# Routed experts of a decoder layer: scattering with accumulation into the output, and both experts' weights staged

## The reference

```python
scores = sigmoid(x @ router)                 # 16 experts, groups of 4, two groups kept
topk_indices = top 2 of scores + e_bias within the two groups
topk_weights = scores[topk] / sum(scores[topk])
a = relu2(x @ w_up[e]) * combine[:, e]       # 512 -> 256
routed = sum over e of a @ w_down[e]         # 256 -> 512
shared = relu2(x @ shared_up) @ shared_down  # 512 -> 1024 -> 512
out = x_residual + routed + shared
```

## Time and profile before

| | |
|---|---|
| Time, median of 3 runs | 1128.84 us (1126.65 to 1132.16) |
| Profiled execution, its own time | 1128.89 us |
| Its span, first to last instruction | 1127.2 us |
| Mean granted TensorE clock | 0.987 |
| Busy: TensorE, VectorE, ScalarE, GpSimd | 94%, 75%, 60%, 58% |
| DMA, mean over the span | 82 GB/s |
| Last down projection of the tile loop ends | 1089.04 us |

### The profile page before, as it was taken

How to read it: one execution, slowest core, us unless ns; L and a number is a source line. 1 busy time by engine, 2 the same in 40 slices (tenths; PEclk the granted TensorE clock), 3 DMA queues, 4 the chain that set the end, 5 groups by cost and what they waited for, 6 DMA issues and landing times.

```text
span 1127.2 us, 19610 instructions
## 1 busy us (share of the span) xinstructions
PE 1060.9 (94%) x6786; PEld 620.4 (55%) x6786; DVE 845.7 (75%) x1297; ACT 676.8 (60%) x1492; POOL 656.7 (58%) x573
## 2 busy tenths in 40 slices
PE   8999988888999999999989889999999999999993
PEld 3554556666666667666666654544444445555541
DVE  6988699999999999999999989840680045545548
ACT  4876789999999899999999944412011022333310
POOL 2022299999999999999999955202043024444420
PEclk9999989999999999999999999999999999999997
DMA  7210001102111111010221007112225523333329
GB/s 225 94 39 21 21 29 39 37 31 76 34 34 30 39 67 39 30 38 31 84 75 31 20 23 278 38 74 75 75 75 206 167 81 122 122 112 123 108 76 381
DMA packets 50865, 92.95 MB, mean 82 GB/s; under 512 B 9294, under 2 KB 17486, under 8 KB 50768
## 3 DMA queue, kind: packets, MB, share of 16 engines
q1 hardware_dynamic: 44368, 72.82, 19.4%
q0 software_dynamic: 6400, 18.88, 5.2%
HBM read 72.67 MB, written 19.01 MB: 81 GB/s over the span
## 4 chain that ended last, share of the span: by engine, by line
PE 71%; POOL 8%; DVE 7%; ACT 7%; issue 5%; DMA 1%; SPq 0%; DVEq 0%; ACTq 0%; POOLq 0%
PE ps L1570 10%; PE ps L2017 7%; PE ps L2029 6%; PE ps L843 6%; POOL w_all L765 5%; PE ps L1584 5%; PE ps L871 4%; PE ps L358 4%; PE ps L832 4%; PE ps L817 4%; DVE w_all L1042 3%; PE ps L310 3%; PE ps L1593 2%; ACT w_all L956 2%; PE ps L882 2%
## 5 line engine op out<-in xcount | busy, mean ns | idle before, releaser
L765 POOL TENSOR_TENSOR w_all<-w_all 128x512 f32<-128x512 f32 x256 | 320.7, 1272 | 20.1 <-DVE w_all L587 14.8
L1042 DVE TENSOR_TENSOR_SCAN w_all<-ps,w_all 128x512 f32<-128x512 f32 x256 | 298.6, 1205 | 1.2 <-ACT ps L939 0.6
L939 ACT ACTIVATE ps<-w_all,low 128x512 f32<-128x512 f32 x256 | 177.6, 697 | 1.0 <-DVE w_all L1042 0.8
L871 PE MATMUL ps<-ident,w_all 128*128 128x128 f32 x1024 | 162.0, 281 | 9.7 <-DVE acc L1050 9.5
L947 ACT ACTIVATE w_all<-ps,low 128x128 f32<-128x128 f32 (+3 forms) x256 | 132.8, 530 | 13.6 <-DVE low L1034 13.6
L871 PEld LDWEIGHTS ps<-ident,w_all 128*128 128x128 f32 x1024 | 114.9, 142 | 34.7 <-issue 20.8
L956 ACT ACTIVATE w_all<-ps 128x256 f32<-128x256 f32 (+2 forms) x192 | 101.9, 531 | 22.9 <-PE ps L832 22.6
L1034 DVE TENSOR_REDUCE low<-ps 128x2 f32<-128x256 f32 (+3 forms) x128 | 103.8, 811 | 14.6 <-PE ps L817 13.9
L1570 PE MATMUL ps<-w_all 128*128 128x512 f32 x256 | 112.1, 594 | 0.0
L832 PE MATMUL ps<-ident,w_all 128*128 128x128 f32 x640 | 108.8, 285 | 1.5 <-ACT low L1013 1.5
L843 PE MATMUL ps<-w_all,low 128*32 128x128 f32 x1280 | 95.0, 278 | 12.1 <-ACT w_all L956 10.8
(11 more groups left out here) (228 smaller groups left out, 1935.2 us busy)
## 6 DMA issues: line engine op xcount, KB each, us to landing
w_all<-b_scratch SPq DMA_DIRECT2D x64, 256.0 KB, 3.2
w_all<-in_w_up SPq DMA_DIRECT2D x16, 512.0 KB, 6.0
w_all<-in_w_down SPq DMA_DIRECT2D x16, 512.0 KB, 7.1
w_all<-sorted_y SPq DMA_DIRECT2D x16, 512.0 KB, 10.5
norms<-attn SPq DMA_DIRECT2D x4, 1024.0 KB, 4.3
out_dram<-acc SPq DMA_DIRECT2D x16, 256.0 KB, 8.8
attn<-in_x SPq DMA_DIRECT2D x3, 1024.0 KB, 6.0
attn<-in_x SPq DMA_DIRECT2D x12, 256.0 KB, 4.3
```

Source lines behind the costliest of these rows:

```text
L765: pool.tensor_tensor(dbu[:, k, :], keep["du"][i // N][:, k * T:(k + 1) * T], b_all[i % 2][:, :], ALU.mult).then_inc(pool_dbu.sem, pool_dbu ...
L871: last = pe.transpose(yb[which][:, k * P:(k + 1) * P], state[i % 2][:, k, t * P:(t + 1) * P], ident[:, :])
L939: act.activation(da[unit % 2][:, :], keep["dt"][i // N][:, k * T:(k + 1) * T], ACT.Exp, scale=keep["a_flat"][:, unit % (N * KD):unit % (N ...
L1042: dve.tensor_tensor_scan(state[i % 2][:, k, :], da[unit % 2][:, :], dbu[:, k, :], 0.0, ALU.mult, ALU.add).then_inc(dve_scan.sem, dve_scan. ...
```

## The change

The output is now written in two steps. First SP stores `acc` (residual and shared experts) of each batch to the output, four transfers of 1 MB, one after another (`store`). Then the y tiles are added to it by GpSimd's accumulating indirect DMAs. Since one tile may hold both pairs of a token, each tile has two scatters: `add_first` adds the rows whose expert is the token's lower one, `add_second` the others, and rows that are not meant are pointed out of bounds. A second scatter waits until the first one of its tile has landed. The late matmuls' result is copied by ScalarE to `acc` of the last batch and added by four plain accumulating DMAs of GpSimd.

The routing weight is now applied to y, as the scale of ScalarE's copy. For that the router sends each pair's weight through the one-hot product too, split into three bf16 pieces (three more planes in `inverse`, a second set of 32 matmuls in `collect`, more small operations in `choose` and `tokens`).

Both units' weights are now staged at fixed places: ScalarE copies the first expert's up weights (with a register load of its own), VectorE the second's up weights and both experts' down weights, with two register loads. TensorE loads no registers. There are four x buffers and four y buffers instead of two of each. Four x loads are issued before the loop instead of two.

```diff
+            def store(b):
+                sp.wait_ge(dve_base.sem, dve_base.upto(4 * b + 3))
+                if b > 0:
+                    sp.wait_ge(s_out.sem, s_out.upto(b - 1))
+                sp.dma_start(d["out"][b, :, :].rearrange("(t p) c -> p t c", p=P),
+                             keep["acc"][:, b, :].rearrange("p (t c) -> p t c", c=D)).then_inc(s_out.sem, s_out.tick(b))
...
             expert(6)
             expert(8)
+            store(0)
...
             expert(11)
+            store(1)
             sp.wait_ge(r["s_routed"], 1)
...
             expert_down(10)
+            store(2)
+            store(3)
             routed["sync"](sp)
...
             pool.wait_ge(s_keep.sem, s_keep.upto(B - 1))
-            for i in range(2):
-                pool.indirect_dma_start(out=r["x_first"][:, i, :], out_offset=None, in_=d["norm_rows"],
+            pool.wait_ge(s_out.sem, s_out.upto(0))
+            for i in range(4):
+                pool.indirect_dma_start(out=r["x_in"][i], out_offset=None, in_=d["norm_rows"],
...
+        for w in range(3):
+            self.link(dve, dve.tensor_tensor(self.weights[:, :, w, :], self.in_tile[:, :, :], over(self.piece[:, w, :], NI), ALU.mult))
         dve.tensor_tensor(self.in_row, over(self.row[:, :], P), each(self.row_id[:, :], P), ALU.is_equal).then_inc(self.s_inverse, 1)
...
-        load(2)
-        load(3)
+        def add_second(i):
+            pool.wait_ge(s_first[i % 2], 16 * (i // 2 + 1))
+            pool.indirect_dma_start(out=out_rows, in_=y[i % YB], in_offset=None, bounds_check=B * T - 1, oob_is_err=False, compute_op=ALU.add,
+                                    out_offset=bass.IndirectOffsetOnAxis(ap=r["second_i"][:, i:i + 1], axis=0))\
+                .then_inc(s_second[i % YB], 16)
+
+        pool.wait_ge(s_out.sem, s_out.upto(B - 1))
         for i in range(SLOT_TILES):
-            if i + 4 < SLOT_TILES:
-                load(i + 4)
-            store(i)
+            add_first(i)
+            if i > 0:
+                add_second(i - 1)
+            if i + XB < SLOT_TILES:
+                load(i + XB)
+        add_second(LAST)
+        for s in range(YB):
+            pool.wait_ge(s_second[s], 16 * ((LAST - s) // YB + 1))
+        for t in range(NT):
+            pool.wait_ge(s_late_copy.sem, s_late_copy.upto(t))
+            pool.dma_start(d["out"][B - 1, t * P:(t + 1) * P, :], late[t], accum_op=ALU.add).then_inc(s_sum, 16)
+        pool.wait_ge(s_sum, 16 * NT)
...
             if main:
-                expert[i] = expert_of(pe, 2 * i)
...
+            if i < LAST:
+                stage_first_up(i + 1)
             if lag:
                 pe_l.wait(act, i - 1, "down")
-                if i >= 3:
-                    act.wait_ge(s_y[s1], (i - 1) // 2 * 16)
-                act_l.done(act.activation(y[s1], bank[6 + s1][:, :], ACT.Copy), "y")
+                if i - 1 >= YB:
+                    act.wait_ge(s_second[(i - 1) % YB], (i - 1) // YB * 16)
+                act_l.done(act.activation(y[(i - 1) % YB], bank[6 + s1][:, :], ACT.Copy, scale=r["w_slot"][:, i - 1:i]), "y")
...
-                    taken[i + 1] = expert_of(dve, 2 * i + 3)
-                    stage_first_half(dve, taken[i + 1], i + 1)
-                stage_second_half(dve, taken[i], i)
+                    taken[i + 1] = [expert_of(dve, 2 * i + 2 + n) for n in range(2)]
+                    stage_second_up(dve, taken[i + 1][1], i + 1)
+                stage_downs(dve, taken[i], i)
         run(step)
-
-        for t in range(TT):
-            dve.wait_ge(s_g[t], before[t] + 16)
...
```

More of the change, by code:

```diff
@@ L1175, in collect @@
         for n in range(2 * B * NT):
-            last = pe.matmul(out[:, 0:2 * SLOT_TILES], self.in_row[:, n, :], self.planes[:, n, :, :].rearrange("p w i -> p (w i)"),
+            pe.matmul(out[:, 0:2 * SLOT_TILES], self.in_row[:, n, :], self.planes[:, n, :, :].rearrange("p w i -> p (w i)"),
+                      start=(n == 0), stop=(n == 2 * B * NT - 1))
+        for n in range(2 * B * NT):
+            last = pe.matmul(out[:, 2 * SLOT_TILES:5 * SLOT_TILES], self.in_row[:, n, :], self.weights[:, n, :, :].rearrange("p w i -> p (w i)"),
                              start=(n == 0), stop=(n == 2 * B * NT - 1))
@@ L1945, in sync @@
     def sync(sp):
-        sp.wait_ge(s_y[0], 16 * (LAST // 2 + 1))
-        sp.wait_ge(s_y[1], 16 * ((LAST + 1) // 2))
-        for t in range(TT):
-            sp.dma_start(back[t], d["sorted_y"][2 * t * P:2 * (t + 1) * P, :].rearrange("(p k) c -> p (k c)", k=2)).then_inc(s_g[t], 16)
-        with sp.Fori(0, B) as b:
-            for t in range(NT):
-                pair.wait(sp, b * NT + t, "second")
-                sp.dma_start(d["out"][b, t * P:(t + 1) * P, :], keep["acc"][:, b, t * D:(t + 1) * D]).then_inc(s_o, 16)
-        sp.wait_ge(s_o, 16 * TT)
+        sp.wait_ge(s_sum, 16 * NT)
     def gpsimd(pool):
@@ L1980, in tensor @@
         pe_l.start(pe)
-        expert = {}
         def turn_x(i):
@@ L2013, in step @@
                     if k % 2 == 0:
+                        act_u.wait(pe, i, f"up{k // 2}")
                         dve_u.wait(pe, i, f"up{k // 2}")
                     for n, rows in enumerate(halves):
[L2016 to L2017 removed]
+                        last = pe.matmul(bank[2 + s][rows, 0:FE], x_t[s][:, k * P + n * HALF:k * P + (n + 1) * HALF], stage_up[n][:, k * FE:(k + 1) * FE],
                                          start=(k == 0), stop=(k == KD - 1))
@@ L2025, in step @@
                 for f in range(FK):
-                    dve_d.wait(pe, i - 1, f"down{f}")
+                    dve_d.wait(pe, i - 1, f"b{f}")
                     for n, rows in enumerate(halves):
-                        w = r["w_all"][:, expert[i - 1], UP + f * D:UP + (f + 1) * D] if n == 0 else stage_down[:, f * D:(f + 1) * D]
-                        last = pe.matmul(bank[6 + s1][rows, :], h_t[:, f * P + n * HALF:f * P + (n + 1) * HALF], w,
+                        last = pe.matmul(bank[6 + s1][rows, :], h_t[:, f * P + n * HALF:f * P + (n + 1) * HALF], stage_down[n][:, f * D:(f + 1) * D],
                                          start=(f == 0), stop=(f == FK - 1))
```

148 lines of the change are left out of this document (88 added, 60 removed).

## The result

The changed kernel takes **1257.63 us** (median of four, 1255.82 to 1263.72) against 1129.03 (1126.65 to 1132.16): 1.115 times the time before, 95% interval 1.110 to 1.119. The forecast was 1181 us, with 1148 to 1214 as its range. The direction held and the size did not: the loss is 129 us, not 52. The profiled execution took 1256.36 us with a span of 1254.6, which is 75.4 us more than the 1179.2 of the forecast's sum.

A forecast was written before the change was run, and what follows sets the result against it. TensorE was taken to pace the loop of 40 tiles, something else the tail. Span 1127.2 - 12 (tail) + 58 (loop) + 6 (before the loop) = 1179.2, plus 1.7 outside it: 1181 us, range 1148 to 1214.

The forecast's parts named there:

- the staging at nothing: Loop: ScalarE's new copies cost nothing, and VectorE's staging is covered at a step of 6.06 us.
- VectorE's round: Loop: relu, square, two register loads and six copies take VectorE 4.5 to 4.9 us a step.
- P of 6.06: Loop: late x stretches the step from 4.40 to 6.06 us; 35 turns x 1.66 = 58 us lost.
- a wait before the turn in each step: Loop: sign that TensorE would wait for the x load in every step, step length near 6.06 us.
- The formula for two steps: Loop: two steps hold one round, 2P = 4.84 + R; with R = 7.28, P is 6.06 us.
- Rival 2: Loop: clock falls as TensorE idles; all steps slow 31 us more, 1212 us, half of them 1197; chance 0.15.
- R = 9.0: Loop, upper bound: scatters 0.5 us longer to issue, x landing 0.7 later; step 6.9 us, 88 us lost.
- The queue against VectorE's copies: Loop: VectorE copies might delay GpSimd's scatter by one or two copies, 7 to 14 us; without that rule nothing.
- The front: Before the loop: products, second matmul set and clock loss add 6 us (5 to 8).
- half, 0.9: Before the loop: idle TensorE may lose clock; half of 1.8 us, 0.9, was taken.
- The tail: After the last down projection: read-backs, VectorE passes and stores go; 26.0 us left, 12 saved (bounds 0 to 13).
- Rival 1: Loop: x in time, R under 4.0; 1123 us, or 1127 to 1143 at VectorE's pace; chance 0.07, 0.04 ending faster.

The follow-up runs named there:

- e1: Changed kernel with the x load of tile i+4 moved ahead of the two scatters in GpSimd's queue; 1165.34 us, 1.031 times the kernel before.
- e5: Kernel before with two GpSimd calls swapped, so its x load stands behind its plain scatter; 1169.23 us, 1.035 times the kernel before.
- e7: Changed kernel with the x load ahead and one plain scatter per tile instead of two adding ones; 1139.27 us, 1.009 times the kernel before.
- e4: Changed kernel with 8 added 128x128 matmuls on TensorE ahead of waits for x; 1216.54 us, 1.078 times the kernel before.
- e2: Changed kernel with both scatters plain, the addition left out; 1213.69 us, 1.074 times the kernel before.
- e9: Changed kernel without GpSimd's own wait for the last four accumulating DMAs; 1256.87 us, 1.111 times the kernel before.

## Why the prediction was right in direction and wrong in size

**What held.** The diagnosis did: the step at fault is the load of x behind two scatters in GpSimd's queue, two steps of the loop hold one round, and R, the time from y written to x landed, sets its length. e1 and e5 show it from both sides, the changed kernel with the load ahead (92 us back) and the kernel before with it behind (40 us lost). In the changed kernel the staging at nothing held: TensorE waited for VectorE's copies twice, 1.9 us in all. At a faster pace it would not be nothing; the 4.5 to 4.9 us that the forecast gave VectorE's round is what e7's first half shows. The second scatter never waited for the first one's landing, and no store of the bases shows in the chain.

**The step that failed** is the forecast's P of 6.06, "58 us lost"; the loop lost 127.5. Its 69.5 us more are two things. There was also a sign in the forecast that did not come: a wait before the turn in each step. The formula for two steps held, but all of their waiting falls into one of them.

*The clock, about 41 us.* Rival 2 named it, priced it at 31 us and gave it 0.15. e4 prices it at 41.0 us. What spoke against it was an argument and not a row: "R runs on while the work is slow, so the idle time shrinks". The chain shows otherwise. R begins with y, and y comes behind the slow projections, in the same round: 1.12 + 3.61 + 2.37, then y, then R. A slow step does not fill the wait, it delays the y on which the next load depends, so the wait stays (4.6 us on average) and the clock falls again. The price was low too. The 1.8 us were read where the clock came back within the down projection; in the round above the slow part costs 0.59 + 1.73 + 0.65 = 2.97 us against the forecast's 0.53, 1.88 and 1.72, in the next one, where the clock comes back earlier, 1.73, and 41 us in 18 rounds are 2.3 on average. The Trainium skill (TensorE: Matmul & The Clock Gate, HAM oscillation) describes just this alternation of a wait for DMA and a slow stretch, and this trace agrees; weighed against one row that showed the fall after a like wait, it should have been the likeliest case.

*R, about 28.5 us.* Term by term, with the forecast's value first and the round of the timeline above second: lead 0.80, 0.77; first scatter 1.02, 1.57; lead of the second 0.80, 0.30; second scatter 1.02, 1.66; gap 0.30, 0.30; x to landed 3.34, 3.64. Together 7.28 against 8.24. The formula with 8.24 gives a round of 13.1, and e4's is 13.0; with the 2.97 of the slow part it gives 16.05, and the round above is 16.14. The forecast took "the row of the same instruction" for a scatter, but an adding one is another instruction: 1.55 us at the least against 1.02, which e2 turns back by taking the adding away. The error of 1.2 for two of them was nearly halved by the second one's lead, 0.50 too long. Beyond this round the loads land later, 4.0 us in the median and 5.0 at most. The loop of e4 is 86.7 us longer than before's, 4.8 us in each of 18 rounds, so its mean round is 8.8 + 4.8 = 13.6: that is 1.5 over the forecast, of which the scatters and leads explain about 0.7. The landing is most of the rest: in e4's chain the loads take 3.2 to 3.4 us from 944 to 1040, as forecast, and 3.8 to 4.9 behind it. Plain scatters bring half a microsecond of it back (e2); why the loads land later in the loop's second half stays open.

**The range.** Both mechanisms stood in the text, one as a bound (R = 9.0) and one as a rival, and the range's upper end, 1214, took each alone. They are not independent: a longer R makes a longer wait, and the wait is what the clock falls after. 1181 + 31 for rival 2 and + 30 for the upper bound of R is 1242, still 16 short, but a range that knew of the pair would have gone there.

**The queue against VectorE's copies.** The forecast left this at up to 14 us. In the changed kernel it is small: the second scatter's median is 1560 to 1570 ns, 1.66 us in the round above. In e1 it is 1712, and halving the copies brings back 1560. A plain scatter has a median of 1.21 to 1.23 us in e7. But to meet a copy is not enough: the first scatter of e2 shown above took 1.01 us, and VectorE's timeline has copies from 1006.37 to 1007.51, across most of it. The Trainium skill (SBUF — State Buffer, Who interferes with whom) has VectorE's copies in a 2-port mode hold a port pair that GpSimd's descriptor writes need. The runs agree that the copies can interfere, by 0.15 to 0.2 us for an issue; that is well under a whole copy, 0.42 to 0.44 us on average in the changed kernel, and e2's scatter shows none of it. Which moment of the issue a copy has to meet wasn't tried.

**The front**, +8.4 against +6. 0.9 us of it lies ahead of the router: TensorE gets to `collect` at 846.19 and not at 845.27, and it was as late at 790.87 (789.96 before) already, which nothing in the profile ties to the change. The wait was 4.2 us against 3.7, since the three products took 6.05 us in all, not 5.6. The two sets of matmuls took 4.4 together, not 1.15 + 1.3: the clock was down behind the wait (0.66 from 850 to 855), and the term "half, 0.9" for that was 2.0. At the loop's start the wait for x is gone.

**The tail**, -8.6 against -12. The late matmuls are 20.81 us as foreseen, the copy 0.60. The missing term is the program's end: GpSimd's DRAIN of 3.50 us begins only when the last accumulating DMA has landed, 1250.9, and the forecast gave 0.4 for everything behind that landing. No row of the kernel before priced it: GpSimd issued its last DMA at 1091.4 and its end lay beside VectorE's passes.

Front, loop and tail together: 2.4 + 69.5 + 3.4 = 75.3, the difference of the spans.

**Rival 1** (x in time) is what e1 comes nearest to, and it too had the wrong pace: not VectorE's 4.5 to 4.9 us but GpSimd's three issues, 1.57 to 1.72 twice, 1.02 and 0.90 of gaps, 5.1 to 5.35 us. With two adding scatters for every tile GpSimd cannot keep up with TensorE's 4.40, in any order of its queue. That is why no version with both scatters tried here beats the kernel before. With GpSimd relieved, in e7, VectorE's round is the next limit, in half of the loop.

## What to carry to other kernels

When an issue is put into a queue, ask for the instruction behind it that feeds the bottleneck, and add up the whole round from there; then put that instruction ahead, which here gave back 92 us and cost nothing, since its buffers were free. Where an estimate leaves a matrix engine waiting for DMA in every round, first work out in which step the waiting gathers, then price that round at the slow clock from the start and do not treat it as a separate, unlikely event. (Here each wait of 3.4 to 5.8 us was followed by a slow step; in e5, with waits of 2.1 us at most, three steps of 40 were slow.) A DMA that computes (adds) is not the DMA in the trace of before: its issue is the first thing to measure, because a queue that was half empty may be full with it.

## What the runs showed of the hardware that was not expected

- Issuing an indirect DMA of 128 rows of 2 KB takes GpSimd 1.01 us without adding and 1.55 us or more with it (e2 against the changed kernel, median 1.57). The plain accumulating DMA of 256 KB takes 0.85 us to issue and lands 4.0 to 4.8 us after its issue began.
- A scatter right behind another one starts after 0.30 us even though it has a wait of its own; the 0.8 us of lead appear only when GpSimd had been waiting for y.
- Matmuls that do nothing useful, 8 of 128 columns in each step ahead of a wait, kept the granted clock at 1.00 and took 41 us off the span.
- In e5 the turns waited 27 times, 25.0 us in all and 2.1 at most (TensorE busy 34.8 of 40 us), and the clock was at 1.00 but for three steps; in the changed kernel, with 18 waits and 82.4 us (busy 27.8 to 29.7 of 40), it fell behind every one of them.
- GpSimd's DRAIN at the end of the program stands behind the wait for its last DMAs and adds 3.5 us to the span of the changed kernel, 1.9 in e2 and 6.9 in e7. Without that wait (e9) it begins with the issue of the last DMA and takes 5.0 us.
